# Cross-attention kernel: maxima of the scores taken two banks at a time, context normalised on GpSimd, one context load and the ternary weights moved

## The reference

```
q = _ln(latents, sa_ln_g, sa_ln_b)
x = latents + _mha(q, q, ...)                     # self-attention, 56 keys
qc, kv = _ln(x, ...), _ln(tokens, ca_kv_ln_g, ca_kv_ln_b)
x = x + _mha(qc, kv, ...)                         # pass 1: 16 heads, 1500 keys
x = _fuse_moe(x, ...)                             # top 2 of 8 experts

Wq' = clip(round(W / (mean|W| + 1e-5)), -1, 1) * mean|W|     # ternary weights
scores = einsum('bqhd,bkhd->bhqk', q, k) * SCALE  # pass 2: the context as it is
probs = softmax(scores)
x = x + (einsum('bhqk,bkhd->bqhd', probs, v) @ Wo' + bo)
```

## Time and profile before

| quantity | value |
|---|---|
| median of 3 runs | 639.55 us |
| profiled execution | 638.79 us |
| its span | 637.0 us |
| PE busy | 544.5 us (85%) |
| DVE busy | 425.6 us (67%) |
| ACT busy | 326.7 us (51%) |
| POOL busy | 152.7 us (24%) |
| mean granted TensorE clock | 0.935 |

### The profile page before, as it was taken

How to read it: one execution, slowest core, us unless ns; L and a number is a source line. 1 busy time by engine, 2 the same in 40 slices (tenths; PEclk the granted TensorE clock), 3 DMA queues, 4 the chain that set the end, 5 groups by cost and what they waited for, 6 DMA issues and landing times.

```text
span 637.0 us, 16158 instructions
## 1 busy us (share of the span) xinstructions
PE 544.5 (85%) x6582; PEld 383.9 (60%) x6582; DVE 425.6 (67%) x1090; ACT 326.7 (51%) x495; POOL 152.7 (24%) x128
## 2 busy tenths in 40 slices
PE   0699838589999999999967989468999999999996
PEld 0587515266766667676745767234666767667674
DVE  5667478679998999977224302569787687786730
ACT  0165214356666576765743333215566567676573
POOL 1554212313241524300015100223041240421000
PEclk9899668889999999999997989878999999999998
DMA  5010733434436353342200642026536436353300
GB/s 154 32 50 1 164 92 69 126 88 110 132 74 172 72 139 75 75 99 50 100 1 1 170 108 66 9 84 146 137 80 175 121 77 168 88 137 75 74 3 15
DMA packets 25338, 57.44 MB, mean 90 GB/s; under 512 B 4660, under 2 KB 8876, under 8 KB 25268
## 3 DMA queue, kind: packets, MB, share of 16 engines
q1 hardware_dynamic: 25268, 56.45, 34.6%
HBM read 17.81 MB, written 0.23 MB: 28 GB/s over the span
## 4 chain that ended last, share of the span: by engine, by line
PE 45%; DVE 23%; issue 21%; DMA 4%; POOL 3%; ACT 2%; SPq 2%; DVEq 0%; POOLq 0%; ACTq 0%
DVE mxp L791 11%; PE SM L1170 10%; PE PO L1185 9%; PE ST L1149 6%; PE MI L1101 6%; DMA cx<-in_ctx 3%; PE MI L1091 3%; DVE cx L779 3%; DVE qst L815 2%; PE MI L1125 2%; PE SM L1257 2%; DVE ksplit L786 1%; DVE cstat L763 1%; PE SM L1125 1%; DVE xn L732 1%
## 5 line engine op out<-in xcount | busy, mean ns | idle before, releaser
L791 DVE TENSOR_REDUCE mxp<-SM 112x1 f32<-112x500 f32 x364 | 235.2, 673 | 60.5 <-PE SM L1170 59.1
L593 ACT ACTIVATE PT<-ST 128x896 f32<-128x896 f32 x192 | 171.1, 911 | 49.7 <-PE ST L1149 49.1
L1170 PE MATMUL SM<-kst,qst 96*112 96x500 bf16 x364 | 143.1, 407 | 24.7 <-DVE mxp L791 24.1
L1149 PEld LDWEIGHTS ST<-qst,kst 98*128 98x128 bf16 x1536 | 95.0, 100 | 32.6 <-issue 9.7
L1149 PE MATMUL ST<-qst,kst 98*128 98x112 bf16 x1536 | 108.5, 215 | 1.2 <-DMA qst<-mrow 1.2
L471 POOL TENSOR_TENSOR kr<-kf,ksplit 128x500 f32<-128x500 f32 x48 | 56.1, 1170 | 184.4 <-ACT ksplit L565 184.3
L1185 PE MATMUL PO<-PT,vaug 125*32 125x112 f32 x3072 | 96.5, 264 | 2.1 <-ACT PT L593 1.5
L1170 PEld LDWEIGHTS SM<-kst,qst 96*112 96x112 bf16 x364 | 46.8, 131 | 66.9 <-DVE mxp L791 55.2
L1185 PEld LDWEIGHTS PO<-PT,vaug 125*32 125x32 f32 x3072 | 70.5, 110 | 24.5 <-issue 14.9
L577 ACT ACTIVATE vaug<-MI 125x512 f32<-125x512 f32 x48 | 28.7, 598 | 79.4 <-PE MI L1101 79.4
L476 POOL TENSOR_TENSOR ksplit<-kr,ksplit 128x500 bf16<-128x500 f32 x48 | 54.5, 1135 | 53.4 <-DVE ksplit L786 53.4
(11 more groups left out here) (129 smaller groups left out, 555.4 us busy)
## 6 DMA issues: line engine op xcount, KB each, us to landing
kst<-ksplit SPq DMA_DIRECT2D x192, 187.5 KB, 3.8
cx<-in_ctx SPq DMA_DIRECT2D x8, 750.0 KB
xT<-in_ctxT SPq DMA_DIRECT2D x8, 750.0 KB, 4.6
moe<-in_w1T SPq DMA_DIRECT2D x8, 256.0 KB, 2.9
moe<-in_w2T SPq DMA_DIRECT2D x8, 256.0 KB, 3.3
qall<-qsplit SPq DMA_DIRECT2D x12, 112.0 KB, 2.3
watt<-in_watt SPq DMA_DIRECT2D x1, 768.0 KB, 5.8
qst<-mrow SPq DMA_DIRECT2D x32, 1.8 KB
```

The lines of the kernel that those rows point to most:

```text
L593: nc.scalar.activation(PT[:, k % PTB], ST[:, k % 2, :, 0:4 * PC], ACT.Exp, scale=SCALE).then_inc(exp_done, 1)
L791: nc.vector.tensor_reduce(mxp[:, j // 3, j % 3:j % 3 + 1], tile_bank(j, banks), AX.X, ALU.max).then_inc(sm_red, 1)
L1149: last = mm(ST[:, k % 2, cc, PC * p:PC * (p + 1)], kst[n.par][:, 4 * half + p, at:at + 128], qst[n.par][:, 4 * half + p], start=True, stop ...
L1170: mm(tile_bank(j, banks), qst[n.par][0:SROWS, j // 3], kst[n.par][0:SROWS, j // 3, at:at + THIRD], start=True, stop=True).then_inc(sm_full, 1)
```

## The change

Four edits.

1. **Max tiles in pairs.** Tiles 2j and 2j+1 are computed one behind the other into the two banks of SM, and one reduction over both (112x2 out of 112x1000) takes their maxima. A unit has 12 such pairs, one in each step (`STEP_MAXES`); in window 0 steps 0, 1 and 10 hold two. In a window pair j waits until the reduction of pair j-1 is done; in `start_pass` pairs alternate between SM and two banks of ST and wait for pair j-2. The pair stands behind the scores and ahead of the values. The maxima of the next item's first half are transposed in step 8 instead of 6 (window 0: 10 instead of 8).
2. **Context normalising on GpSimd**: the 12 instructions of windows 0 to 4 of pass 1 follow the power on GpSimd; VectorE's next aggregate waits until they are done.
3. **Context load.** The call stands at the end of the window for item n+4 instead of at the head for n+3; item 3 is loaded ahead of the experts' first weights.
4. **Ternary weights** are made in window 5 of pass 1, behind step 6's reduction.

```diff
+MAXES = TILES // 2
+START_MAXES = 9
-STEP_TILES = spread_tiles(0, (3, 3, 3, 2, 2, 2, 2, 2, 1, 1, 2, 1))
-OWN_MX_STEP, NEXT_MX_STEP = 1, 6
+STEP_MAXES = spread_maxes(0, (1,) * STEPS)
+OWN_MX_STEP, NEXT_MX_STEP = 1, 8
+FIRST_MAXES = spread_maxes(MAXES - START_MAXES, (2, 2, 1, 1, 1, 1, 1, 1, 1, 1, 2, 1))
+FIRST_OWN_MX_STEP, FIRST_NEXT_MX_STEP = 3, 10
...
+        def max_banks(j, pairs):
+
+            if j % pairs < pairs - 1:
+                return ST[0:PC, 1, :, 0:THIRD]
+            return SM[0:PC, :, 0:THIRD]
...
-                if n.s == 0 and (n + 3).exists():
-                    load_ctx(n + 3)
...
+                if n.s == 0 and (n + 4).exists():
+                    load_ctx(n + 4)
...
             restack(u0, 1)
+            load_ctx(Unit(0, None, 3))
             load_expert(0, 0)
...
+            def ctx_normalise(n):
+
+                pool.wait_ge(crstd_ready, n.count(1, 1))
+                for i in range(3):
+                    for c in range(CPT * i, CPT * (i + 1)):
+                        last = nc.gpsimd.tensor_scalar(cx[n.par][:, c], cx[n.par][:, c], cmv[:, c, 0:1],
+                                                       crstd[:, c:c + 1], ALU.subtract, ALU.mult)
+                    last.then_inc(cn_ready, 1)
...
-                dve.wait_ge(sm_full, n.count(TILES, j + 1))
-                nc.vector.tensor_reduce(mxp[:, j // 3, j % 3:j % 3 + 1], tile_bank(j, banks), AX.X,
-                                        ALU.max).then_inc(sm_red, 1)
+                dve.wait_ge(sm_full, n.count(MAXES, j + 1))
+                nc.vector.tensor_reduce(mxp[:].rearrange("q p i -> q (p i)")[:, 2 * j:2 * j + 2],
+                                        max_banks(j, pairs), AX.X, ALU.max).then_inc(sm_red, 1)
...
+                    if n.s == 0 and n.c == B - 3 and k == HSTEP:
+                        ternary_weights()
...
                         if k == 5:
+                            if ln_unit.it is not None or ln_unit.c > 3:
+                                dve.wait_ge(cn_ready, (ln_unit + -1).count(3, 3))
                             ctx_aggregate(ln_unit)
-                        if k in (7, 8, 9):
-                            ctx_normalise(ln_unit, (k - 7,))
...
-                wait(pe, sm_red, n.count(TILES, j + 1 - banks))
-                at = THIRD * (j % 3)
-                mm(tile_bank(j, banks), qst[n.par][0:SROWS, j // 3], kst[n.par][0:SROWS, j // 3, at:at + THIRD],
-                   start=True, stop=True).then_inc(sm_full, 1)
+                wait(pe, sm_red, n.count(MAXES, j + 1 - pairs))
+                for i in range(2):
+                    p, at = (2 * j + i) // 3, THIRD * ((2 * j + i) % 3)
+                    last = mm(max_banks(j, pairs)[:, i], qst[n.par][0:SROWS, p], kst[n.par][0:SROWS, p, at:at + THIRD],
+                              start=True, stop=True)
+                last.then_inc(sm_full, 1)
```

More of the change, by code:

```diff
@@ L111, in first, with maxes @@
         return self.it is None and self.c == 0
-    def tiles(self, k):
+    def maxes(self, k):
         if not (self + 1).exists():
             return []
-        return FIRST_TILES[k] if self.first() else STEP_TILES[k]
+        return FIRST_MAXES[k] if self.first() else STEP_MAXES[k]
     def mx_steps(self):
@@ L836, in add_projection, with ternary_weights @@
                                         ).then_inc(x_added, 1)
+            def ternary_weights():
+                dve.wait_ge(gam_ready, 1)
+                nc.vector.tensor_scalar(thr[:, 0], gam[:], EPS, 0.5, ALU.add, ALU.mult)
+                nc.vector.tensor_scalar(thr[:, 1], gam[:], EPS, -0.5, ALU.add, ALU.mult).then_inc(thr_ready, 1)
+                dve.wait_ge(thr_ready, 1)
+                for w in range(4):
+                    nc.vector.tensor_scalar(wt[:, 0, w], watt[:, 2, w], thr[:, 0, w:w + 1], None, ALU.is_gt)
+                    last = nc.vector.tensor_scalar(wt[:, 1, w], watt[:, 2, w], thr[:, 1, w:w + 1], None, ALU.is_lt)
+                last.then_inc(tern1, 1)
+                dve.wait_ge(tern1, 1)
+                nc.vector.tensor_tensor(wt[:, 0], wt[:, 0], wt[:, 1], ALU.subtract).then_inc(tern2, 1)
+                dve.wait_ge(tern2, 1)
+                for w in range(4):
+                    last = nc.vector.scalar_tensor_tensor(out=wt[:, 1, w], in0=wt[:, 0, w], scalar=gam[:, w:w + 1],
+                                                          in1=watt[:, 2, w], op0=ALU.mult, op1=ALU.subtract)
+                last.then_inc(tern3, 1)
+                dve.wait_ge(tern3, 1)
+                nc.vector.tensor_tensor(watt[:, 2], watt[:, 2], wt[:, 1], ALU.add).then_inc(wq_ready, 1)
             def window(n):
@@ L955, in start_pass @@
                 place_q(first, 0)
-                for j in range(START_TILES):
-                    reduce_tile(first, j, banks=4)
-                    if j == 3:
+                for j in range(START_MAXES):
+                    reduce_maxes(first, j, pairs=2)
+                    if j == 1:
                         place_q(first, 1)
-                    if j == START_TILES - 2:
+                    if j == START_MAXES - 1:
                         place_q(first + 1, 0)
-                    if j in (1, 4, 7):
-                        k_second_part(first + 1, j // 3)
-                    if j == TILES // 2 - 1:
+                    if j in (0, 2, 3):
+                        k_second_part(first + 1, (0, 2, 3).index(j))
+                    if j == MAXES // 2 - 1:
                         max_parts(first, 0)
@@ L1158, in scores, with max_tiles @@
                     output_forth(n + -1)
-            def max_tile(n, j, banks=2):
+            def max_tiles(n, j, pairs=1):
                 if j == 0:
@@ L1200, in window @@
                     scores(n, k)
-                    tiles = [(n + ahead, j) for ahead, j in n.tiles(k)]
-                    if tiles:
-                        max_tile(*tiles[0])
+                    maxes = [(n + ahead, j) for ahead, j in n.maxes(k)]
+                    if maxes:
+                        max_tiles(*maxes[0])
                     if k % 2 == 0 and (k or prv.exists()):
@@ L1207, in window @@
                         values(of, (k - 1) % STEPS)
-                    for tile in tiles[1:-1]:
-                        max_tile(*tile)
                     if 0 <= k - K_STEP < 3 and k_unit.exists():
@@ L1313, in start_pass @@
                 first = Unit(s, None, 0)
-                for j in range(START_TILES):
-                    max_tile(first, j, banks=4)
-                    if j in (1, 4, 7):
-                        prev = project_v(first, j // 3, prev)
-                    if s == 0 and j in (10, 13, 16):
-                        prev = transpose_ctx(first + 2, (10, 13, 16).index(j), prev)
-                    if j == TILES // 2 + 3:
+                for j in range(START_MAXES):
+                    max_tiles(first, j, pairs=2)
+                    if j in (0, 2, 3):
+                        prev = project_v(first, (0, 2, 3).index(j), prev)
+                    if s == 0 and j in (5, 6, 8):
+                        prev = transpose_ctx(first + 2, (5, 6, 8).index(j), prev)
+                    if j == MAXES // 2 + 1:
                         transpose_max(first, 0)
```

62 lines of the change are left out of this document (20 added, 42 removed).

## The result

The changed kernel takes 682.0 us (median of 4 runs, 677.2 to 685.0), the kernel before 640.1 beside it (637.7 to 642.9): a ratio of 1.065, 95% interval 1.056 to 1.073. The forecast was 652 with a range of 634 to 665. The direction was right, the size, +42 measured against +13, was not. The profiled execution has a span of 675.4 us and a granted clock of 0.923 (before 637.0 and 0.935).

The account below looks back on a forecast made before the run. TensorE was taken to bound pass 2's steady windows, TensorE and VectorE, both full, those of pass 1. Pass 1 -2.0 and pass 2 +14.8 gave +12.8 on the profiled 638.79: 651.6, forecast as 652 us, range 634 to 665.

Parts of the forecast that it names:

- Pairs, price of one: VectorE's two-bank reduction: 1.19 us, between 0.67 and 1.35; pairs make VectorE 1.1 us less busy in a window.
- the new wait: Pair j waits for pair j-1's reduction: a loop of 1.90 us per step; five late steps cost 9.5, +3.55.
- The rival of a free single buffer (a): Single pair buffer costs nothing, TensorE finds its banks free; windows stay at 25.5, total time 623 us; chance 0.15.
- Early steps of pass 2: Pair 0 to pair 7 in a steady window: 17.7 us against 19.6, -1.9; the whole window 27.2, +1.7.
- Rival (b): Early steps give more back, no waits for MI in steps 1 and 3: total time 640 us; chance 0.12.
- Pass 1: the step that failed: Steady windows of pass 1, bound as pass 2's plus 0.3 for three transposes: 27.5 us, -0.35 in each of four.
- the three terms of pass 2: Pass 2: four steady windows +6.8, the windows of 23.2 and 19.7 +4, window 0 +4; together +14.8.
- Rival (c): GpSimd normalising is slow: at 1.14 us each the total time is 679, at 0.8 it is 664; chance 0.11.
- my threshold model: GpSimd normalising in pass 1 costs nothing up to about 0.6 us each, then 12 x the excess in five windows.
- Context load: Item 3's load ahead of the experts' weights returns the 5.51 us wait and the clock: 8.6 us in window 0.
- rival (d): Item 3's load isn't needed early, or queries' DMAs suffer: 5 us less gain, 657; inside the forecast's 0.62 chance.
- Ternary weights: Moved from the start to window 5 of pass 1: gain 0.5 at the start, +2.5 in window 5, net +2.0.

Follow-up runs that it names:

- the two kernels where the lower clock lasts longer: Ternary weights in window 5 alone on the kernel before, 645.3 us; the changed kernel with context normalising back on VectorE, 677.0 us.

## Why the prediction was wrong

**Pairs, price of one and the new wait: right.** Reduction 1.196 us (forecast 1.19), loop 1.92 (1.90), waits behind pairs 7, 9 and 11 of 0.76, 0.90 and 0.99, late steps 9.7 (9.5). The rival of a free single buffer (a) fell.

**Early steps of pass 2: mis-sized.** I let them give back 1.9 us; they gave back 1.1. A window went up by 2.7, not by 1.7. That lies at the high end of my own bounds (2.8), but by luck: that end stood for a reduction of 1.35 us, and it took 1.20. In the early steps no pair waits for its banks, and the waits for MI (0.51 and 0.23) are no longer than I put them (0.55 and 0.4). What was too small is TensorE's own work: each of the seven intervals is longer than priced, by up to 0.19 us, mostly the pair, 0.46 to 0.53 from its start to the next instruction where I had 0.42. The late steps add the other 0.2. Over four windows, +3.9; windows 5 and 6 +1.4; window 0 of pass 2 +4.6, where 15 pairs meet the loop and the granted clock is 0.80. Rival (b), more given back, went the wrong way.

**Pass 1: the step that failed.** "With VectorE eased, a window of pass 1 is bound as one of pass 2 plus 0.3 for three transposes: 27.5." It measured 29.93. Of the missing 2.4, 1.0 is that pass 2's window is itself 28.2, 0.75 is context work that isn't hidden (29.29 with the pairs alone, where the sum gives 28.5), and 0.64 is GpSimd. I took TensorE alone to bound the window once VectorE had 3.1 us less to do; with the loop neither is full (26.3 and 21.9 of the 29.9 us), and the two wait for each other in turn. With a clock dip in one window this stage missed by 11.1 of the 25.6 us that the span missed; the three terms of pass 2 together missed by 9.9.

**GpSimd: the premise failed, the consequence was covered.** The forecast priced it at nothing "up to about 0.6 each"; it takes 0.797 in a run of twelve, so scaling the 500-column row by length, to 0.29, was wrong; its full 1.14, my high end, was nearer. Rival (c) stood at 664 for 0.8 us each, +12 over the forecast; beside the pairs it costs about 4 us in the four windows, without them 22. So my threshold model, 12 x the excess, erred both ways (and its 679 for 1.14 us each didn't follow it: 12 x 0.54 is 6.5 us a window, not 5.5), because the cover it compares with is set by the pace of the other steps.

The Trainium skill (GPSIMD Engine Reference, Elementwise — side-by-side cycle accounting) gives a best case of 1.8 cycles an element at 1.2 GHz plus dispatch, by which I had worked out 0.19 us for the loop alone. The trace has 0.797 for 128 columns and 1.14 for 500 in two-input form, which suggests that most of a short instruction is not its elements; the two forms differ, and no run varies the length of one.

**Context load: direction right, rival (d) half right.** Window 0 saves 7.55 us by the load alone (forecast 8.6), but the queries wait 2.36 us for their DMA. I counted the queue order and not the 750 KB that then stand before the weights.

**Ternary weights: right in size in the changed kernel, by luck** (+2.3 in window 5, forecast +2.5): the same block costs +5.8 and +6.1 in the two kernels where the lower clock lasts longer.

What stays open: the clock's dips. The changed kernel's runs spread over 677 to 685 us and its window 0 of pass 2 is 3.9 us longer than that of the pairs alone, with the same instructions there and a granted clock of 0.80 against 0.89. In the steady windows and windows 5 the dips come in or behind waits of TensorE, of 4.1 and 3.05 us for the ternary block, of 1.7 and less for GpSimd's thirds or for pairs. Why one such wait is followed by a dip and a like one is not, and why one dip lasts 3.3 us and another 17, these runs don't show. Open too is what an even spread with its exchange in step 8 and two alternating banks would cost: no run has it.

## What to carry to other kernels

Before two small operations are merged, look whether they alternated between buffers: the merged one runs in a loop of writer plus reader, and its price is that loop in every step whose own work is shorter. Keep work where the other steps have slack, and when work is spread anew, move what reads its results too: here 1.05 us of the 1.63 that an even spread cost was a wait for maxima that had become late. Price a move to a slow engine by the distance between the producer's start and the first reader that waits, measured on the trace, and again after every other edit, since that distance is what the other edits change.
